# Delta-rule stage of a two-block transformer: triangular inverses in two diagonal blocks with the block below made on TensorE, idle matmuls taken out, and a residual addition moved to TensorE

## The reference

```python
def step(S, ch):
    Q, K, V, bt = ch
    Kb = K * bt
    Vb = V * bt
    A = jnp.eye(C, dtype=dt) + jnp.tril(jnp.einsum('bhcd,bhed->bhce', Kb, K), -1)
    T = solve_triangular(A.astype(jnp.float32), jnp.broadcast_to(I32, A.shape), lower=True).astype(dt)
    W = T @ Kb
    U = T @ Vb
    St = S.swapaxes(-1, -2)
    mid = U - W @ St
    O = Q @ St + jnp.einsum('bhcd,bhed->bhce', Q, K) * M @ mid
    S_new = S + mid.swapaxes(-1, -2) @ K
    return (S_new, O)
```

## Time and profile before

| | us |
|---|---|
| median of 3 runs | 1620.83 (1619.78 to 1622.5) |
| the profiled execution | 1622.98 |
| its span, first to last instruction | 1621.2 |
| PE busy in the span | 1348.3 (83%) |
| DVE busy | 1283.6 (79%) |
| ACT busy | 863.6 (53%) |

### The profile page before, as it was taken

The page is one execution under the profiler, slowest core; times in us unless marked ns, Lnnn a source line. Parts: engine busy times, 40 slices in busy tenths (PEclk is TensorE's granted clock), DMA queues, the critical chain, the costliest instruction groups (busy, mean ns, idle before and its releaser), DMA issues. The chain is left out here.

```text
span 1621.2 us, 37551 instructions
## 1 busy us (share of the span) xinstructions
PE 1348.3 (83%) x13383; PEld 991.3 (61%) x13383; DVE 1283.6 (79%) x2864; ACT 863.6 (53%) x1583; POOL 116.8 (7%) x76
## 2 busy tenths in 40 slices
PE   0679998999999999999989999437777776778786
PEld 0566776777777777777757777325554544556665
DVE  6886117998989898989987888387778783899997
ACT  0565235777767776777757777211212211666664
POOL 2000000000000000000021222200000000221221
PEclk9868999999999999999998999757889889888888
DMA  8000002433434333333322555632222001011110
GB/s 235 1 0 0 5 4 81 121 120 117 118 112 123 116 115 117 117 118 117 119 73 75 147 155 149 214 118 81 82 82 81 30 30 61 27 58 58 59 48 30
DMA packets 122285, 142.44 MB, mean 88 GB/s; under 512 B 8768, under 2 KB 78752, under 8 KB 121120
## 3 DMA queue, kind: packets, MB, share of 16 engines
q1 hardware_dynamic: 118704, 134.81, 27.1%
q10 hardware_dynamic: 3440, 5.79, 1.0%
HBM read 106.49 MB, written 34.08 MB: 87 GB/s over the span
## 5 line engine op out<-in xcount | busy, mean ns | idle before, releaser
L1008 ACT ACTIVATE glu_a<-moe_a,b1s 128x512 f32<-128x512 f32 x256 | 176.5, 689 | 150.4 <-PE moe_a L910 121.9
L1013 ACT ACTIVATE b_raw<-moe_b,b1s 128x512 f32<-128x512 f32 x256 | 176.5, 689 | 0.8 <-PE moe_b L910 0.6
L1061 DVE TENSOR_TENSOR glu_a<-glu_a,gate_row 128x512 f32<-128x512 f32 x256 | 174.9, 683 | 0.0
L1053 DVE SCALAR_TENSOR_TENSOR glu_a<-glu_a,b_raw 128x512 f32<-128x512 f32 x256 | 174.8, 683 | 0.1
L908 PE MATMUL moe_a<-x_hi,w_hi 128*128 128x512 f32 x256 | 148.2, 579 | 5.4 <-DVE w_lo L1070 5.4
L1044 DVE TENSOR_SCALAR b_raw<-b_raw 128x512 f32<-128x512 f32 x256 | 108.1, 422 | 56.3 <-ACT b_raw L1013 54.2
L928 PE MATMUL moe_y<-glu_a,w2s 128*128 128x512 f32 x256 | 132.0, 596 | 2.6 <-DVE glu_a L1061 2.5
L910 PE MATMUL moe_b<-x_hi,w_lo 128*128 128x512 f32 x256 | 101.2, 395 | 0.0
L910 PE MATMUL moe_a<-x_hi,w_lo 128*128 128x512 f32 x256 | 101.0, 394 | 0.0
L909 PE MATMUL moe_b<-x_lo,w_hi 128*128 128x512 f32 x256 | 100.4, 392 | 0.0
L909 PE MATMUL moe_a<-x_lo,w_hi 128*128 128x512 f32 x256 | 100.3, 392 | 0.0
(11 more groups left out here) (266 smaller groups left out, 3080.6 us busy)
## 6 DMA issues: line engine op xcount, KB each, us to landing
gate_row<-gate_scratch SPq DMA_DIRECT2D x256, 256.0 KB, 3.2
kq_in<-kq_scratch SPq DMA_DIRECT2D x8, 1024.0 KB, 7.2
acc<-in_L_attn_inputs SPq DMA_DIRECT2D x8, 512.0 KB, 10.0
kq_scratch<-q_out SPq DMA_DIRECT2D x16, 256.0 KB, 2.9
xq_scratch<-qT SPq DMA_DIRECT2D x16, 256.0 KB, 2.0
v_scratch<-v_out SPq DMA_DIRECT2D x16, 256.0 KB, 2.3
k_scratch<-k_out SPq DMA_DIRECT2D x16, 256.0 KB, 2.8
k_rows_scratch<-k_rows SPq DMA_DIRECT2D x16, 256.0 KB, 3.2
```

The costliest lines, as they stand in the source:

```text
L1008: act.activation(glu_a[e % 4][:, :], ps_a[u][:, :], ACT.Gelu_apprx_sigmoid, bias=w["b1"][:, 0, e:e + 1]).then_inc(a_glu, 1)
L1013: act.activation(b_raw[u][:, :], ps_b[u][:, :], ACT.Identity, bias=w["b1"][:, 1, e:e + 1])\
L1053: dve.scalar_tensor_tensor(a, a, GLU_LIMIT, b_raw[u][:, :], ALU.min, ALU.mult)\
L1061: dve.tensor_tensor(a, a, gate_row[e % 4][:, :], ALU.mult).then_inc(weighted, 1)
```

## The change

In `delta_pass` each 32x32 inverse is made in blocks of BL = 16. DVE eliminates the two diagonal blocks together, 15 columns with 2 x (15-j) x (j+1) elements a partition, in the same buffers with a stride. The block below the diagonal is made by two products on PE: ACT copies gram's corner into `below` beside lt; `turn_n` (DVE) transposes the first diagonal block's inverse into dn; `cross` (PE, 128 products with 16 columns) forms below x dn in ps_c; `keep_half` (ACT) copies it to half_way; `join` (PE, 128 more) multiplies with the second diagonal block's inverse out of tt; `fix` (DVE) subtracts the result from tt and raises t_ready. `turn_t` comes before join and no longer stands at a group's end. cross and join of group g+1 stand at places 4 and 5 of PE's order in group g. The tables become LATE_AT (columns 8 to 14 of g+1, places 0 to 4) and SOON_AT (columns 0 to 7 of g+2, places 8 to 15). `stay_awake` and its buffers go. In `finish_pass`, the addition of acc becomes a product of acc with the identity into the same ps_f, and `finish` a copy on ACT.

```diff
@@ -1474,9 +1474,16 @@
-        lower = [sb(f"lower{i}", [P, CH, CH]) for i in range(2)]
-        tinv = [sb(f"tinv{i}", [P, CH, CH]) for i in range(2)]
-        prod = [sb(f"solve_prod{i}", [P, CH, CH]) for i in range(2)]
+        BL = CH // 2
+        STRIDE = BL * CH + BL
+        lower_flat = [sb(f"lower{i}", [P, 2 * STRIDE]) for i in range(2)]
+        tinv_flat = [sb(f"tinv{i}", [P, 2 * STRIDE]) for i in range(2)]
+        prod = [sb(f"solve_prod{i}", [P, 2, BL, BL]) for i in range(2)]
+        below = [sb(f"below{i}", [P, NCH, CH]) for i in range(2)]
+        dn = sb("dn", [P, NCH, BL])
+        half_way = sb("half_way", [P, NCH, CH])
...
-        idle_in, ps_idle, idle_set = sb("idle_in", [P, 512], BF16), ps("dl_idle", [P, 512]), sem("idle_set")
+        ps_c = ps("dl_c", [P, NCH, BL])
...
-        HALF = 11
-        SOLVE = 2 * (CH - 1)
-        ALONE_AT = {1: 3, 2: 1, 5: 3, 6: 1, 7: 1}
+        HALF = 8
+        SOLVE = 2 * (BL - 1)
+        LATE_AT = {0: 2, 1: 1, 2: 2, 3: 1, 4: 1}
+        TURN_N_AT, TURN_T_AT, FIX_AT = 5, 6, 12
         TAKE_AT = {1: 0, 3: 1, 5: 2, 7: 3}
-        PAIRS_AT = {9: 4, 10: 1, 11: 1, 13: 4, 14: 1}
-        LAST_AT = {k: (3, 1, 1)[k % 4 - 1] for k in range(16) if k % 4}
+        SOON_AT = {k: 1 for k in range(8, 16)}
+        CROSS_PLACE, JOIN_PLACE = 4, 5
...
@@ -1583,17 +1604,39 @@
-                    for _ in range(times):
-                        pe.matmul(ps_idle[:, :], idle_in[:, 0:P], idle_in[:, :], start=True, stop=True)
+                def cross(g):
+                    pe.wait_ge(lt_copied, 2 * QUARTERS * (g + 1))
+                    pe.wait_ge(dn_ready, g + 1)
+                    if g == 0:
+                        pe.wait_ge(blanked, 3)
+                    else:
+                        pe.wait_ge(t_ready, g)
+                    for n in range(NCH):
+                        for rows in heads():
+                            mm = pe.matmul(ps_c[rows, n, :], below[g % 2][rows, n, :], dn[rows, n, :],
+                                           start=True, stop=True)
+                    mm.then_inc(crossed, 1)
+                def join(g):
+                    pe.wait_ge(dt_ready, g + 1)
+                    wait_before_product(pe, passed, half_ready, g + 1)
+                    for n in range(NCH):
+                        for rows in heads():
+                            mm = pe.matmul(ps_c[rows, n, :], half_way[rows, n, :], tt[g % 2][rows, n, BL:],
+                                           start=True, stop=True)
+                    mm.then_inc(joined, 1)
                 def scan(g):
                     def while_waiting(place):
-                        stay_awake(3 if place % 2 else 2)
                         if g + 2 < GROUPS and place in GRAM_PLACES:
...
                             gram(g + 2, GRAM_PLACES[place])
+                        if g + 1 < GROUPS and place == CROSS_PLACE:
+                            cross(g + 1)
+                        if g + 1 < GROUPS and place == JOIN_PLACE:
+                            join(g + 1)
                     for c in range(CG):
                         at = [g * STEPS + 2 * c + h for h in range(2)]
@@ -1621,7 +1664,6 @@
                                     mm = pe.matmul(ps_m[h][rows, b, :], tt[g % 2][rows, n, :], r[h][rows, b, :],
                                                    start=True, stop=True)
                             mm.then_inc(mid_done, 1)
-                        stay_awake(2)
                         for h in range(2):
                             wait_before_product(pe, passed, mid_ready, at[h] + 1)
                             for b in range(HB):
...
@@ -1643,15 +1686,29 @@
+                        if g >= 2:
+                            act.wait_ge(crossed, g - 1)
+                    if g == 0:
+                        act.wait_ge(blanked, 3)
                     for quarter in quarters:
                         act.wait_ge(grammed, QUARTERS * g + quarter + 1)
+                        act.activation(below[g % 2][:, 8 * quarter:8 * quarter + 8, BL:],
+                                       ps_g[quarter % 2][:, :, 0, BL:], ACT.Copy,
+                                       scale=w["upper"][:, 1, BL - 1:BL]).then_inc(lt_copied, 1)
                         act.activation(lt[:, :, 8 * quarter:8 * quarter + 8].rearrange("p c n -> p n c"),
                                        ps_g[quarter % 2][:, :, 0, :], ACT.Copy).then_inc(lt_copied, 1)
+                def keep_half(g):
+                    act.wait_ge(crossed, g + 1)
+                    if g >= 1:
+                        act.wait_ge(joined, g)
+                    act.activation(half_way[:, :, 0:BL], ps_c[:, :, :], ACT.Copy).then_inc(half_ready, 1)
                 def scan(g):
                     if g >= 2:
...
                             copy_gram(g + 2, GRAM_PLACES[2 * c])
+                        if g + 1 < GROUPS and 2 * c == CROSS_PLACE:
...
+                    m, n = j + 1, BL - 1 - j
                     if j > 0:
                         dve.wait_ge(solve[g % 2], SOLVE * (g // 2) + 2 * j)
-                    dve.tensor_tensor(prod[g % 2][:, m:, 0:m], lower[g % 2][:, m:, j:m].to_broadcast([P, n, m]),
-                                      tinv[g % 2][:, j:m, 0:m].to_broadcast([P, n, m]), ALU.mult)\
+                    dve.tensor_tensor(prod[g % 2][:, :, m:, 0:m],
+                                      lower_blocks[g % 2][:, :, m:, j:m].to_broadcast([P, 2, n, m]),
+                                      tinv_blocks[g % 2][:, :, j:m, 0:m].to_broadcast([P, 2, n, m]), ALU.mult)\
                        .then_inc(solve[g % 2], 1)
                 def subtract(g, j):
                     m = j + 1
                     dve.wait_ge(solve[g % 2], SOLVE * (g // 2) + 2 * j + 1)
-                    dve.tensor_tensor(tinv[g % 2][:, m:, 0:m], tinv[g % 2][:, m:, 0:m], prod[g % 2][:, m:, 0:m],
-                                      ALU.subtract).then_inc(solve[g % 2], 1)
+                    x = tinv_blocks[g % 2][:, :, m:, 0:m]
+                    dve.tensor_tensor(x, x, prod[g % 2][:, :, m:, 0:m], ALU.subtract).then_inc(solve[g % 2], 1)
...
+                def turn_n(g):
+                    dve.wait_ge(solve[g % 2], SOLVE * (g // 2 + 1))
+                    if g >= 1:
+                        dve.wait_ge(crossed, g)
+                    dve.transpose(dn[:, :, :].rearrange("p n s -> p s n"),
+                                  tinv[g % 2].rearrange("p i c -> p c i")[:, 0:BL, :]).then_inc(dn_ready, 1)
                 def turn_t(g):
-                    dve.wait_ge(solve[g % 2], SOLVE * (g // 2 + 1))
                     if g >= 2:
                         dve.wait_ge(mid_done, STEPS * (g - 1))
-                    dve.transpose(tt[g % 2][:, :, :].rearrange("p n i -> p i n"), tinv[g % 2][:, :, :])\
-                       .then_inc(t_ready, 1)
+                    dve.transpose(tt[g % 2][:, :, :].rearrange("p n i -> p i n"), tinv[g % 2]).then_inc(dt_ready, 1)
+                def fix(g):
+                    dve.wait_ge(joined, g + 1)
+                    x = tt[g % 2][:, :, BL:]
...
@@ -1763,27 +1836,29 @@
                 def scan(g):
                     late, soon = g + 1, g + 2
-                    alone = iter(range(HALF, CH - 1))
-                    beside = iter(range(HALF))
+                    last = iter(range(HALF, BL - 1))
+                    first = iter(range(HALF))
                     for k in range(4 * CG):
                         if k % 4 < 2:
                             residue(g, k // 4, k % 2)
                         else:
                             update(g, k // 4, k % 2)
+                        if late < GROUPS:
+                            for _ in range(LATE_AT.get(k, 0)):
+                                eliminate((late, next(last)))
+                            if k == TURN_N_AT:
+                                turn_n(late)
+                            if k == TURN_T_AT:
+                                turn_t(late)
+                            if k == FIX_AT:
+                                fix(late)
                         if soon < GROUPS:
-                            for _ in range(ALONE_AT.get(k, 0)):
-                                eliminate((late, next(alone)))
                             if k in TAKE_AT:
                                 take_gram(soon, TAKE_AT[k])
                                 if TAKE_AT[k] == QUARTERS - 1:
                                     turn_gram(soon)
-                            for _ in range(PAIRS_AT.get(k, 0)):
-                                eliminate((late, next(alone)), (soon, next(beside)))
-                        elif late < GROUPS:
-                            for _ in range(LAST_AT.get(k, 0)):
-                                eliminate((late, next(alone)))
-                    if late < GROUPS:
-                        turn_t(late)
+                            for _ in range(SOON_AT.get(k, 0)):
+                                eliminate((soon, next(first)))
```

(44 more changed lines are left out.)

11 lines of the change are left out of this document (9 added, 2 removed).

## The result

The changed kernel takes 1708.15 us, median of 4 runs (1707.31 to 1712.88); the kernel before took 1621.66 beside it. The ratio is 1.054 (95% interval 1.052 to 1.056): 86.5 us slower, where I forecast 65 us slower. The profiled execution's span is 1705.5 us instead of 1621.2.

What follows compares the result with a forecast made beforehand. The scan was taken to be bound by fetching PE's 256-instruction blocks, about 3.75 us each, the last pass by DVE. Terms +105 - 34 - 0.8 + 4.5 - 9.5 gave +65 us, 1686 us; 8-in-10 range 1662 to 1724.

Steps and rivals of the forecast that it cites:

- blocks of 256 instructions: PE's instruction supply in the delta stage: each block costs the larger of 3.75 us and its own work with waits.
- 95 packets: Sign in the delta stage's DMA view: instruction packets should rise from 66 to about 97.
- Added products: Cross and join on PE in the scan: 4.0 blocks a group, 15.0 us, so +105 us for seven groups.
- The rest of a group: Other scan work: with DVE relieved and no longer late, 31.2 instead of 36.0 us a group, -34 us.
- Idle matmuls: Scan's eighth group: 28 removed pairs save 0.2 block, -0.8 us.
- the low clock: Rival for the scan: without idle matmuls PE's clock falls, +20 to +45 us on the sum, about 1719; chance 0.14.
- Ahead of the scan: Before the first dl_m: shorter elimination, but cross(0) and join(0) stand ahead; +4.5 us, between +1 and +8.
- Last pass: Result addition moves from DVE to PE and ACT, 0.69 us a tile over 16 tiles: -9.5 us, between -12 and -3.
- 239: Sign in the last pass: its stretch should take 239 us or so.
- The faster rival: Scan: fetch doesn't bind, DVE does; products cost 8.2 us of PE work a group, -27 us, 1594 us; chance 0.05.
- The one-pair rival: Cross and join: each small product is one pair, costing 2 blocks a group, 52 us less, 1634 us; chance 0.05.
- 4096 pairs: Sign in PE's dl_c rows (cross and join): 4096 pairs expected; 2048 would prove the prediction wrong.

Runs made afterwards that it cites:

- the wide products: Changed kernel with cross and join as 32 or 4 products each instead of 128, same columns, most blocks wrong: 1614.46 and 1605.29 us.
- the join loop: Changed kernel with most of cross and join as four loop passes over the same 32 small products, plus wide ones, most blocks wrong: 1656.71 us.
- 4 wide products: Changed kernel with cross and join as 4 products of 512 columns each instead of 128 small ones, only one chunk's block right: 1605.29 us.

## Why the prediction was right, and which terms were off

The side, the mechanism and the range held. The size came nearer than its two large terms: the price of the products was put 15.5 us too high and the relief by DVE 30 us too high, and the two errors partly cancel. That was luck. Step by step:

- **"PE's program arrives in blocks of 256 instructions, and the next block is not there sooner than about 3.7 us after the last one was entered."** Shown: by the stalls inside the cross and join batches, 95 packets (I had said about 97), the wide products (-94 and -103 us for the same columns), and the join loop that runs without a stall. The figure is a mean, not a floor: in the changed kernel's scan the shortest distance between stalls is 3.34 us and the median 3.96.
- **Added products, +105 us.** Mis-sized: 12.8 us a group, 89.5 for seven, measured both by adding them to the kernel before and by taking them out of the changed one. I multiplied four whole blocks by 3.75 and they cost 3.2 each; that a part of PE's work and waits of before goes on beside the fetch is my explanation, which no run tests.
- **The rest of a group, -34 us.** This is the term that failed. It measured -0.5 us a group, -4 us in all, inside its bounds (0 to -47) but far from the value I took. I reasoned that DVE's work delayed many blocks and that without it a group would fall near the floor of its 7.8 blocks, 29.3 us. DVE's work did fall, by 8.5 us a group where I had said 9.4. But PE had waited only 19.1 us for DVE in the whole scan of before, which I didn't set against my 34. And what it no longer waits for DVE it waits for its blocks: of the two kernels without idle matmuls and without the added small products, the one with the full elimination has 26.7 us of waits for DVE in the scan and 63.1 under "issue", the one with half of it and 4 wide products about 19 and 71, and their groups are 35.72 and 35.50 us. The elimination, 18.5 us of DVE's time a group, stood almost wholly beside PE's own work and stalls; taking half of it away freed DVE and not the group. That the floor is not reached has a reason in the trace of before that I passed over. I took a block to cost the larger of 3.75 us and its work with waits. The block ahead of the one that the earlier trace rows begins with, in PE's timeline:

```profile
1342.68 0.24 PE L1610 MATMUL dl_s<-kq_in,ST 32*32 32x64 f32 x1 [0.64 <-issue]
1342.85 0.60 PE L1589 MATMUL dl_idle<-idle_in 128*128 128x512 bf16 x2
1344.09 1.02 PE L1621 MATMUL dl_m<-r,tt 32*32 32x32 f32 x64 [0.63 <-DVE r L1747]
1345.03 0.60 PE L1589 MATMUL dl_idle<-idle_in 128*128 128x512 bf16 x2
1345.57 1.02 PE L1630 MATMUL dl_s<-ak,mid 32*32 32x64 f32 x57
```

PE enters this block at 1342.68, waits for DVE until 1344.09, is through with its 126 pairs at 1346.59, and still stands until 1348.11: 5.43 us after the entry, but 4.02 after the wait's end. The instruction packets of the trace tell more. The packet for the next block starts at 1345.62, 2.94 us after the entry, and PE goes on 2.49 us after that. For the block entered at 1348.11 the packet starts at 1349.37, 1.26 us after the entry, and PE goes on 2.39 us later. In the changed kernel's scan, all 77 stalls of at least 0.4 us end 2.2 to 2.9 us after the last packet's start, whatever the work; the packet itself starts between 1.0 and 4.1 us after PE entered the block, and in three of four cases less than 1.8. So a block is long where its fetch starts late, and in such a block waits and fetch add up instead of covering each other. What starts a fetch isn't shown: the early wait for DVE fits the case above, but other late packets stand behind no wait of PE that the timeline shows (the changed kernel's block entered at 1292.92 has its packet 4.1 us later), and no run here moved a wait inside a block to test it.

- **Idle matmuls, -0.8 us in the last group.** It measured +4.4: the clock did cost there, and in the seven other groups it did not show. As a rival the low clock had 0.14 and +20 to +45 us. It is refuted as the cause of the excess, by the matmuls put back (no gain at a clock of 0.78) and by the kernel before without them (1.0004).
- **Ahead of the scan, +4.5.** Measured +3.2; the two kernels with wide products start 12.6 and 12.2 us earlier than the changed one, which is what the small products of cross(0) and join(0) cost beyond the wide ones.
- **Last pass, -9.5.** Measured -8.9 in the span and -9.6 (-12 to -7) alone. The stretch of 249 us began 5.9 us behind the scan's end; the same stretch is 240.3 us now, where I had named 239.
- The sum of terms, +65, against +84.3 in the span (+86.5 by the medians): -15.5 for the products, +30 for the rest of the groups, +5 in the last group and -1 in the small terms.
- The faster rival is refuted: its price for the products (8.2 us of work a group) was near the 7.0 us that they take in the loop, but written out they cost 12.8. The one-pair rival fell with the 4096 pairs.
- The Trainium skill ("Runtime: NRT & Kernel Launch", Instruction fetch mechanics) says that the fetch is hidden because the sequencer issues more slowly than the blocks arrive. These traces don't agree for PE with short matmuls: 128 pairs, 256 instructions, are through in 1.25 us and the next block lets PE go on 3.73 us after the last.

## What to carry to other kernels

Where PE runs long stretches of small matmuls without a loop, count instructions as you count columns: here 256 of them, 64 fp32 products, took 3.3 us at the least and mostly about 4, however little they compute. Look for "issue" gaps at a constant number of instructions and for the packets of the instruction queue; if they are there, moving work from DVE to PE in many small products loses, and fewer, wider products or a loop gain. And before an engine's relief is booked, look at how long the others waited for it: DVE was busy 76% of the scan, PE waited for it 19.1 us of 274, and half of its elimination was worth some half a microsecond a group.

## What was not expected of the hardware

- A loop body that is already there runs without fetches: 256 pairs in 3.49 us, 13.6 ns each, against 3.4 to 3.8 us for 126 written out.
- In the changed kernel's scan PE went on 2.2 to 2.9 us after an instruction packet's start in all 77 stalls of 0.4 us or more. Long blocks were those whose packet started late.
- The distance between stalls is the same at 1.2 GHz (3.46, 3.74 us) and at 2.4 GHz (3.73 us).
- The scan's granted clock fell from 0.86 to 0.64 when the idle matmuls went, and the time did not move (ratio 1.0004).
- An fp32 pair of 128x128 with 64 columns took 215 ns at 1.2 GHz, in a row of 128, against 30 ns for a 32x32 pair with as many columns at that clock (64 in 1.93 us).
